# Expert rows of a mixture of experts in 25 whole tiles and 11 tiles of two 64-row units, instead of 39 whole tiles

## The reference

```python
gate = rmsnorm(x) @ wg_W + wg_b + (genre_embed @ gg_W + gg_b)
gate_w = softmax(gate)
topk_w, topk_i = top_k(gate_w, 2)
h1 = relu(x @ W1[e] + b1[e])       # 256 -> 512, for each expert e
h2 = relu(h1 @ W2[e] + b2[e])      # 512 -> 512
out_e = h2 @ W3[e] + b3[e]         # 512 -> 256
out = sum over the token's two experts of weight * out_e
```

## Time and profile before

| | us |
|---|---|
| time of the kernel, median of 3 runs | 798.35 (797.91 to 800.69) |
| the profiled execution, its own time | 798.27 |
| its span in the profile | 796.5 |
| PE busy | 753.0 (95%) |
| DVE busy | 496.9 (62%) |
| ACT busy | 278.9 (35%) |
| POOL busy | 80.9 (10%) |
| granted TensorE clock, mean | 0.979 |

### The profile page before, as it was taken

How to read it: one execution, slowest core, us unless ns; L and a number is a source line. 1 busy time by engine, 2 the same in 40 slices (tenths; PEclk the granted TensorE clock), 3 DMA queues, 4 the chain that set the end, 5 groups by cost and what they waited for, 6 DMA issues and landing times.

```text
span 796.5 us, 23084 instructions
## 1 busy us (share of the span) xinstructions
PE 753.0 (95%) x9468; PEld 657.4 (83%) x9468; DVE 496.9 (62%) x1090; ACT 278.9 (35%) x838; POOL 80.9 (10%) x91
## 2 busy tenths in 40 slices
PE   4489999999999999979999999999999999999786
PEld 2389989999999999967778878977897789778675
DVE  4664574444444445235688778777877787778756
ACT  3022212212211221234446435633563455336420
POOL 2221101111111100010000000000000000000000
PEclk8699999999999999989999999999999999999989
DMA  9878343111111113200000000000000000000000
GB/s 321 278 253 266 118 180 100 34 35 41 40 35 34 41 29 106 74 28 21 22 22 10 28 28 16 16 29 28 9 21 29 28 9 21 29 8 15 8 9 15
DMA packets 29686, 48.53 MB, mean 61 GB/s; under 512 B 3307, under 2 KB 19435, under 8 KB 29069
## 3 DMA queue, kind: packets, MB, share of 16 engines
q1 hardware_dynamic: 20432, 32.47, 12.0%
q0 software_dynamic: 3408, 9.31, 4.0%
q10 hardware_dynamic: 5741, 5.27, 2.0%
HBM read 39.82 MB, written 7.22 MB: 59 GB/s over the span
## 4 chain that ended last, share of the span: by engine, by line
PE 88%; DVE 6%; ACT 1%; issue 1%; another core or an unknown queue 1%; DMA 1%; POOL 1%; DVEq 0%; ACTq 0%; POOLq 0%
PE ps L611 17%; PE ps L686 15%; PE ps L600 8%; PE ps L623 8%; PE ps L763 7%; PE ps L709 7%; PE ps L731 4%; PE ps L783 3%; PE ps L754 2%; PE ps L724 2%; PE ps L814 2%; PE ps L795 2%; PE ps L861 2%; PE ps L829 2%; PE ps L878 2%; PE ps L851 1%
## 5 line engine op out<-in xcount | busy, mean ns | idle before, releaser
L611 PE MATMUL ps<-h_t,w_now 128*128 128x128 f32 x1248 | 145.9, 275 | 1.0 <-DVE h_t L1322 1.0
L611 PEld LDWEIGHTS ps<-h_t,w_now 128*128 128x128 f32 x1248 | 142.4, 192 | 1.5 <-issue 1.4
L686 PE MATMUL ps<-arena,l_weights 128*128 128x128 f32 x1024 | 128.5, 280 | 0.5 <-ACT arena L1017 0.5
L686 PEld LDWEIGHTS ps<-arena,l_weights 128*128 128x128 f32 x1024 | 122.0, 195 | 2.0 <-ACT arena L1017 0.9
L979 ACT ACTIVATE h_t<-ps,cols 128x128 f32<-128x128 f32 x156 | 44.4, 367 | 215.0 <-PE ps L600 187.0
L1313 DVE COPY w_now<-arena 128x2048 f32 x39 | 47.8, 1227 | 104.5 <-PE ps L611 100.7
L1023 ACT ACTIVATE arena<-ps,cols 128x128 f32<-128x128 f32 x256 | 72.9, 370 | 20.8 <-PE ps L686 20.8
L600 PEld LDWEIGHTS ps<-xg_t,w_now 128*128 128x128 f32 x624 | 75.3, 192 | 4.8 <-DVE w_now L1305 2.1
L600 PE MATMUL ps<-xg_t,w_now 128*128 128x128 f32 x624 | 76.4, 276 | 2.3 <-ACT xg_t L970 2.0
L623 PE MATMUL ps<-arena,h_t 128*128 x312 | 73.8, 379 | 0.0
L495 POOL DMA_INDIRECT xg<-in_x,slot_tok x39 | 45.3, 1163 | 232.0 <-PE ps L590 204.3
(11 more groups left out here) (245 smaller groups left out, 1008.2 us busy)
## 6 DMA issues: line engine op xcount, KB each, us to landing
arena<-in_w SPq DMA_DIRECT2D x16, 512.0 KB
arena<-in_w SPq DMA_DIRECT2D x8, 1024.0 KB
expert_out<-y ACTq DMA_DIRECT2D x39, 128.0 KB
arena<-in_x_t SPq DMA_DIRECT2D x2, 1024.0 KB, 6.1
arena<-in_x SPq DMA_DIRECT2D x16, 128.0 KB, 2.5
out<-arena SPq DMA_DIRECT2D x16, 128.0 KB, 1.7
b<-in_b SPq DMA_DIRECT2D x1, 1024.0 KB, 13.5
l_weights<-in_wq SPq DMA_DIRECT2D x1, 1024.0 KB
```

The source lines that it names most:

```text
L611: last = mm(ps[:, 2, m * P:(m + 1) * P], w2_now[:, k, m * P:(m + 1) * P], h1_t[j % 2][:, k, :], start=k == 0, stop=k == KM - 1)
L686: last = mm(ps[:, b, c * P:(c + 1) * P], wt[:, k, f:f + P], m_t[:, k, :], start=k == 0, stop=k == KH - 1)
```

## The change

A slot list of 36 tiles takes the place of 39. 25 tiles (`FULL`) hold 128 rows of one expert each. What is left of each expert (under 128 rows) is padded to a multiple of 64 and goes to 11 mixed tiles (`MIXED`) of two 64-row units, each with an expert of its own. The mixed tiles stand at positions 10 to 20 of the order of work; 15 whole tiles follow them. `mixed(p)`, `nth(p)` and `slot_tile(p)` translate positions.

In a mixed tile the 64 rows of a unit are stationary and the weights move: the units occupy the two halves of the array's columns, and each half gets its own expert's weights. The result has rows on the partitions, so:

- PE has two more groups of four transposes in each mixed tile (`turn_h1`, `turn_h2`);
- DVE adds the bias as a row (`add_b1`, `add_b2`, 512 columns) before the transposes, and copies W1 and W2 twice, once for each unit; b1 and b2 rows come by two more indirect DMAs for each mixed tile, issued by POOL;
- ACT does both ReLUs as one instruction each after the transposes (`relu1`, `relu2_mixed`), and copies W3 twice (`take_w3`), 1024 columns each.

The extra buffers lie where the attention weights will be, so these are now loaded only after the last mixed tile. DVE's planning has more arithmetic, part of it issued without a wait after each instruction (`step.go`), and side stage 1 on DVE has eight more small instructions. In whole tiles too, DVE now waits for PE first and then fetches the expert number.

```diff
-SLOT_TILES = (TOPK * TOK + EXP * (P - 1)) // P
+UNIT = 64
+UNITS = P // UNIT
+FULL = -(-(TOPK * TOK - EXP * (P - 1)) // P)
+MIXED = -(-(TOPK * TOK - FULL * P + EXP * (UNIT - 1) - (UNIT - 1)) // P)
+SLOT_TILES = FULL + MIXED
+FIRST_MIXED = EXP + 2
+LAST_MIXED = FIRST_MIXED + MIXED - 1
...
+            sp.wait_ge(y_ps, LAST_MIXED + 1)
             for dst, name in ((wq, "wq"), (wk, "wk"), (wv, "wv"), (wo, "wo")):
...
             def layer1(j):
...
+                if mixed(j):
+                    for k in range(KH):
+                        for g in range(UNITS):
+                            part_ = slice(g * UNIT, (g + 1) * UNIT)
+                            last = mm(ps[part_, 0, :], xg_t[:, k, part_], w1_of[g][:, k, :],
+                                      start=k == 0, stop=k == KH - 1, tile_position=(0, g * UNIT))
+                    last.then_inc(l1_ps, 1)
+                    return
...
+            def turn_h1(j):
+                pe.wait_ge(h1r_set, nth(j) + 1)
+                if nth(j):
+                    pe.wait_ge(h1t_set, j)
+                for m in range(KM):
+                    last = pe.transpose(ps[:, 1, m * P:(m + 1) * P], h1_rows[:, m * P:(m + 1) * P], ident[:, :])
+                last.then_inc(h1r_turned, 1)
...
             def layer3(j):
...
+                if mixed(j):
+                    pe.wait_ge(h2m_set, nth(j) + 1)
+                    pe.wait_ge(y_set, j)
+                    pe.wait_ge(w3_set, nth(j) + 1)
...
+                if mixed(j - 1):
+                    turn_h2(j - 1)
                 if exists(j, SLOT_TILES):
                     layer2(j)
+                if mixed(j + 1):
+                    turn_h1(j + 1)
...
+            def relu2_mixed(j):
+                act.wait_ge(h2r_turned, nth(j) + 1)
+                act.wait_ge(y_ps, j - 1)
+                f(h2_t[j % 2][:, :, :], ps[:, 3, :].rearrange("p (k q) -> p k q", k=KM), ACT.Relu).then_inc(h2m_set, 1)
+
+            def take_w3(j):
...
+                act.wait_ge(y_ps, j)
+                for g in range(UNITS):
+                    e = act.value_load(row_expert[g * UNIT:g * UNIT + 1, nth(j):nth(j) + 1], min_val=0, max_val=EXP - 1)
+                    at = act.snap(e * E_SIZE + W3_AT)
+                    last = act.copy(w3_now[g].rearrange("p k n -> p (k n)"), arena[:, bass.ds(at, KM * HID)])
+                last.then_inc(w3_set, 1)
+
             def expert_step(j):
-                if exists(j + 1, SLOT_TILES):
+                if mixed(j - 1):
+                    take_w3(j - 1)
+                if exists(j + 1, SLOT_TILES) and not mixed(j + 1):
                     relu1(j + 1)
                 if exists(j + 2, SLOT_TILES):
                     copy_x(j + 2)
+                if mixed(j - 1):
+                    relu2_mixed(j - 1)
+                if mixed(j + 1):
+                    relu1(j + 1)
...
             def take_w1(j):
+                if j:
+                    dve.wait_ge(l1_ps, j)
+                if mixed(j):
+                    if nth(j) == 0:
+                        dve.wait_ge(setup_done, 1)
+                        dve.wait_ge(fa_stored, 16)
+                        dve.wait_ge(moe_loaded, 48 * EXP)
+                    for g in range(UNITS):
+                        at = dve.snap(unit_expert(j, g) * E_SIZE + W1_AT)
+                        last = dve.tensor_copy(w1_of[g][:, :, :].rearrange("p k n -> p (k n)"), arena[:, bass.ds(at, KH * MID)])
+                    last.then_inc(w1_set, 1)
+                    return
                 e = expert(j)
                 at = dve.snap(e * E_SIZE + W1_AT)
                 dve.wait_ge(moe_loaded, 48 * (e + 1))
-                if j:
-                    dve.wait_ge(l1_ps, j)
...
+                if mixed(j + 1):
+                    add_b1(j + 1)
                 if exists(j + 2, SLOT_TILES):
                     take_w1(j + 2)
...
+                if mixed(j):
+                    add_b2(j)
                 if exists(j + 1, SLOT_TILES):
                     take_w2(j + 1)
-                if exists(j, SLOT_TILES):
+                if exists(j, SLOT_TILES) and not mixed(j):
                     relu2(j)
```

More of the change, by code:

```diff
@@ L81, in exists, with mixed, nth, slot_tile @@
     return not isinstance(t, int) or 0 <= t < n
+def mixed(p):
+    return FIRST_MIXED <= p <= LAST_MIXED
+def nth(p):
+    return p - FIRST_MIXED if mixed(p) else p if p < FIRST_MIXED else p - MIXED
+def slot_tile(p):
+    return FULL + nth(p) if mixed(p) else nth(p)
 def later(t):
@@ L97, in __call__, with go, done @@
         self.n += 1
+        self.engine.wait_ge(self.sem, self.base + self.n)
+    def go(self, instruction):
+        instruction.then_inc(self.sem, 1)
+        self.n += 1
+    def done(self):
         self.engine.wait_ge(self.sem, self.base + self.n)
@@ L216, in build @@
         f_hid = r(KH, BATCH)
-        f_a, f_b, f_c = (r(HID, parts=BATCH) for _ in range(3))
+        f_a, f_b = (r(HID, parts=BATCH) for _ in range(2))
         f_s = r(8, parts=BATCH)
@@ L1254, in _ @@
-            tt(back, rest, first_slot, ALU.subtract).then_inc(dve_step, 1)
-            step.n += 1
-            step(tt(picked, rank, rest, ALU.subtract))
-            step(stt(picked, picked, float(P), back, ALU.is_lt, ALU.mult))
-            step(tt(rank, rank, picked, ALU.subtract))
-            for c in range(TOPK):
-                step(tt(picked, rank, mask[c], ALU.mult))
-                step(red(slot_f[:, c, :], picked, X, ALU.add))
+            first_row, seg_of = excl[:, :, 0], [seg[:, n * EXP:(n + 1) * EXP] for n in range(3)]
@@ new lines, in _ @@
+            from_of = [seg_from[:, n * EXP:(n + 1) * EXP] for n in range(3)]
+            step(tt(count_i, incl[:, :, TT - 1], first_row, ALU.subtract))
+            step.go(ts(full_i, count_i, -P, None, ALU.bitwise_and))
+            step(ts(up_i, count_i, float(UNIT - 1), None, ALU.add))
+            step.go(ts(seg_of[0], full_i, float(P), None, ALU.min))
+            step(ts(up_i, up_i, -UNIT, None, ALU.bitwise_and))
+            step.go(tt(seg_of[1], full_i, seg_of[0], ALU.subtract))
+            step(tt(seg_of[2], up_i, full_i, ALU.subtract))
@@ new lines, in _ @@
+            step.go(tt(to_rest, to_rest, jump, ALU.subtract))
+            step(tt(over_first, over_first, per_e(to_full), ALU.mult))
+            step.go(tt(over_full, over_full, per_e(to_rest), ALU.mult))
+            step(tt(rank, rank, over_first, ALU.add))
+            step(tt(rank, rank, over_full, ALU.add))
+            for c in range(TOPK):
+                step.go(tt(picked[c], rank, mask[c], ALU.mult))
+            step.done()
+            for c in range(TOPK):
+                step.go(red(slot_f[:, c, :], picked[c], X, ALU.add))
@@ L1326, in add_b3 @@
             def add_b3(j):
+                if mixed(j):
+                    dve.wait_ge(y_ps, j + 1)
+                    dve.wait_ge(y_stored, 16 * j)
+                    for g in range(UNITS):
+                        part_ = slice(g * UNIT, (g + 1) * UNIT)
+                        e = dve.value_load(row_expert[g * UNIT:g * UNIT + 1, nth(j):nth(j) + 1], min_val=0, max_val=EXP - 1)
+                        last = tt(y[part_, :], ps[part_, 4, 0:HID], b3[part_, bass.ds(e * HID, HID)], ALU.add)
+                    last.then_inc(y_set, 1)
+                    return
                 e = expert(j)
```

200 lines of the change are left out of this document (160 added, 40 removed).

## The result

The changed kernel takes 800.81 us (median of 20 runs, 799.66 to 804.06), the kernel before on the same chip 798.62 (20 runs): a ratio of 1.0029, 95% interval 1.0019 to 1.0040. It is 0.3% slower, 2.2 us, where 1.8 us less had been forecast. The profiled execution took 800.11 us with a span of 798.4. The time lies inside the range of 790.5 to 802.5 us that was given; the direction is the other. Where two times are compared in us without a word on how, the difference is that of the medians.

The account below looks back on a forecast made before the run. PE was taken to bound the kernel, the expert stage being PE alone. The terms -21.9 + 13.9 + 2.9 + 2.3 + 1.0 = -1.8 us on 798.27 us gave 796.5 us, range 790.5 to 802.5.

Parts of the forecast that it names:

- three whole tiles: Expert stage, bound by PE alone: three tiles fewer at 7.30 us each, -21.9 us.
- 11 mixed tiles: PE in mixed tiles: 8.56 us each, 1.26 more than a whole one, +13.9 us (10.6 to 17.4).
- fetch behind the wait, second copies: DVE's W1 and W2 copies, where PE already waits for DVE: +2.9 us, between 0 and 4.
- leaving the mixed tiles: Last mixed tiles: ACT's queue delays mixed ReLU 2, so PE waits before layer 3, +1.1 and +1.2: 2.3 us (0 to 3).
- planning: DVE's planning before the first expert tile: net +1.0 us, of it 1.7 for sixteen instructions without a wait; -0.7 to +3.9.
- the first W1: DVE's first copy of W1, with its fetch now behind the wait: +0.15 us.
- In step 9 W2 is copied twice ahead of ReLU 2 ... +0.5: First mixed layer 2: ReLU 2 ready 4.8 us after the previous layer 2, against PE's 4.3: +0.5 us.
- rival of an array that empties fully at each change: Changes between tiled and full products on PE drain the array: +13.2 us, 809.7 us; chance 0.005.
- Step 0: First expert step: ReLU 2 delayed by the fetch +0.75, first W1 +0.15, together 0.9 us.
- Costs nothing in steady state: Whole tiles: the fetch behind the wait delays ReLU 2 by 0.75 us, inside DVE's spare 0.93, so no cost.
- ACT did not set the pace of the mixed tiles: Rival: ACT's chain from store to ReLU 2 paces mixed tiles; 804.2 us at 1.0 us more; chance 0.11.
- The waits did not find cover: Rival: the waits are hidden, leaving three tiles, mixed tiles and planning: -7.0 us, 791.3 us; chance 0.28.

Follow-up runs that it names:

- tiles_37: The kernel before with 37 tiles instead of 39, leaving out two tiles empty for this input: 785.69 us, 0.9825 of the kernel before.
- three_fixes: Changed kernel with expert number fetched before the wait, mixed ReLU 2 first on ACT, mixed tiles at 14 to 24: 791.65 us, 0.9904 of the kernel before.
- after_again: The changed kernel, unchanged, run again on a second chip: 796.48 us against 795.25 for the kernel before, 1.0007.
- before: The kernel before, unchanged, on the chip of the result: 798.62 us.
- before_again: The kernel before, unchanged, for a second profile, on the second chip: 795.23 us in one run, against a median of 795.25.
- after: The changed kernel in its first measurement, that of the result: 800.81 us, 1.0029 of the kernel before.
- after_third: The changed kernel, unchanged, on a third chip: 800.77 us against 799.65 for the kernel before, 1.0027.
- after_fourth: The changed kernel, unchanged, on a fourth chip: 802.32 us, 1.0036 of the kernel before.
- after_fifth: The changed kernel, unchanged, as a control in a later set of runs: 796.08 us against 796.30 for the kernel before, 0.9993.
- after_sixth: The changed kernel, unchanged, as the control on a further chip: 795.62 us against 796.52 for the kernel before, 0.9983.
- fetch_first: The changed kernel with the expert number fetched before the wait on PE, for W1 and W2: 792.82 us, 0.9964 of the kernel before.
- at_14_again: The changed kernel with mixed tiles at positions 14 to 24, repeated in a later set of runs: 793.89 us, 0.9969 of the kernel before.
- the edit that it implied: The changed kernel with ACT's mixed ReLU 2 ahead of the next whole tile's ReLU 1 and the copy of x: 798.46 us, 0.9989 of the kernel before.
- mixed_at_14: The changed kernel with mixed tiles at positions 14 to 24 instead of 10 to 20, third chip: 796.98 us, 0.9968 of the kernel before.
- the burst that was made on purpose twice: Changed kernel, mixed tiles at 14, POOL's first b1 gather held until layer 2 of tile 12: 793.12 us (0.9967), then 792.82 us (0.9952).
- before_wait_first: The kernel before with DVE waiting for PE first and fetching the expert number after, in both copies: 797.55 us, 1.0025 of the kernel before.
- warm_36: The changed kernel with 36 instead of 24 dummy matmuls at its start: 799.84 us against 800.02 for the kernel before, 1.0010.
- four_fixes: Changed kernel with fetch before wait, mixed ReLU 2 first, mixed tiles at 14, 36 dummy matmuls: 788.82 us, 0.9900 of the kernel before.

## Why the prediction was wrong

By its own steps, from profiles without the late release at the first mixed tile:

| step | forecast | measured | from |
|---|---|---|---|
| three whole tiles | -21.9 | -21.9 | `tiles_37`, 7.31 each |
| 11 mixed tiles | +13.9 | +14.8 | `three_fixes`, tiles 12 to 26 |
| fetch behind the wait, second copies | +2.9 | +3.4 | intervals of layer 2, below |
| leaving the mixed tiles | +2.3 | +2.6 | `three_fixes` against `after_again` |
| planning | +1.0 | +0.5 | gate to slot table, below |
| sum | -1.8 | -0.6 | |

On these three chips the ratios mean +0.6, -0.6 and -1.4 us, each with an interval of about 1 us or more to either side; their average of -0.5 agrees with the sum, but doesn't prove it. On the other three they mean +2.2 to +2.9 us. The profiles allow a sharper comparison, since the span can be cut at the gate's first result, the first layer 2 and the first attention scores (times in us):

| profile | to the gate's result | to the first layer 2 | to the first scores | to the end |
|---|---|---|---|---|
| `before` | 13.5 | 32.0 | 296.4 | 454.6 |
| `before_again` | 13.5 | 31.8 | 296.4 | 451.6 |
| `after` | 15.7 | 32.6 | 297.5 | 452.6 |
| `after_third` | 15.9 | 32.7 | 297.5 | 452.7 |
| `after_fourth` | 16.2 | 32.0 | 299.3 | 454.8 |
| `after_again` | 16.3 | 31.3 | 296.9 | 451.4 |
| `after_fifth` | 16.0 | 32.8 | 295.5 | 451.2 |
| `after_sixth` | 15.6 | 31.2 | 295.5 | 451.7 |

All of the forecast but the planning (and 0.15 us for the first W1) lies in the column to the first scores: -21.9 + 13.9 + 2.9 + 2.3 = -2.8 us. Measured are -0.9 us (`after_fifth`, `after_sixth`; +0.4 in `after_again`, with its last interval of 9.02) without the late release and +1.1 (`after`, `after_third`) with it. The release is worth 2.0 us there and turns the sign of this stage. The profiled pair of the result, 1.9 us apart in span, is then 2.16 (slow first products) + 0.58 (planning and first tile) + 1.10 (expert stage) - 1.94 (attention stage). The last goes with the granted clock, which differs between executions of the same code: in the 12 us from the first scores it is 0.72 in `before` and in `after_fourth`, 0.86 in `after`, `after_third` and `before_again`.

**The step that failed** is "Together 0.9 + 2.0 = 2.9 us; between 0, if all of it found cover, and 4", in its last part, "In step 9 W2 is copied twice ahead of ReLU 2 ... +0.5". It took for granted that DVE resumes 0.40 us after PE's layer 2, so that the copy, with its fetch, starts at T + 1.15. So it does in `after_again` (T + 1.18), where PE's wait is 0.33 us against 0.5 forecast. But in half of the sets of runs, that of the result among them, the copy starts at T + 3.07 and PE waits 2.20 us. Of the 4.0 us by which the forecast was off, 1.9 are this; the rest is in sizes, below, and in what varies from execution to execution. The rows of before had a warning that I quoted for another purpose: the group of line 1045 in the earlier trace rows shows "remote 6.2" of idle time on ACT. That is this kind of lateness, at the start of the attention stage. It cost the kernel before 1.7 us (3.11 against 1.38 us of waiting on PE in `before` and `before_again`), and I didn't ask whether the change could meet another.

The other sizes, in the order of the sum:

- *Mixed tiles.* The steady tile is right (8.56 forecast, 8.56 to 8.57 measured). The 0.9 us more are the passages between tiles of the two kinds, for which I used the steady price. The prediction's rival of an array that empties fully at each change would have cost 13.2 us more; these runs have room for less than 1, so for this kernel it is out. The Trainium skill, "TensorEngine Tiling (Array Packing)", section "Key Properties", says that a change of the tiling mode drains TensorE; whatever drain there is, is in the 0.16 us of the earlier trace rows.
- *Fetch behind the wait, second copies.* The fetch's part is shown by two opposite edits. Step 0 cost 0.6 (0.9 forecast). Behind the side stages the intervals of layer 2 to tiles 8, 9 and 10 grew by 0.5, 1.7 and 1.15 us, of which 1.0 belongs to the mixed tiles themselves: 2.4 against 2.0. Between `after_again` and `fetch_first` the three shrink by 0.8, 0.05 and 0.4, so the fetch accounts for about half of the 2.4. The rest is the second copies while DVE is late from the side stages: in `at_14_again`, with the mixed tiles elsewhere, the intervals to tiles 9 and 10 are back at 7.38 and 7.32 us. The last step of the stage added 0.4 (1.7 in one execution), and I had counted nothing for it. "Costs nothing in steady state" was right, but the last steps are not steady: DVE has the attention stage's work in them.
- *Leaving.* Named with its place and cause, and removed by the edit that it implied.
- *Planning.* Sized too high. The slot table, before and after:

```profile
31.97 0.20 DVE L1282 CAST slot_tok<-ps 128x39 int32<-128x39 f32 x1 [0.29 <-PE ps L570]
```

```profile
34.61 0.20 DVE L1453 CAST slot_tok<-ps 128x36 int32<-128x36 f32 x1 [0.35 <-PE ps L643]
```

From the gate's first result that is 31.97 - 13.52 = 18.45 us and 34.61 - 15.68 = 18.93: 0.5 us. It is the same in every other profile (18.92 to 18.95 with the change, 18.45 and 18.46 before). Sixteen instructions without a wait cost less than the 1.7 us that I took. The first layer 1, forecast about 1 us later, came at 42.41 instead of 39.75, 2.7 us later, but 2.2 of these are the slow first products.

Two rivals are decided. ACT did not set the pace of the mixed tiles; it has the 0.2 us to spare. The waits did not find cover, and `fetch_first` shows what it would have been worth.

**What stays open.** Why a release comes late at these two places on some chips was not settled: in `mixed_at_14`, on such a chip, the first mixed layer 2 has no such wait, so it hangs on the place or on what goes on beside it, and the burst that was made on purpose twice met chips that don't show it. With 1.9 us added to -0.6 the sum is +1.3, against +2.2 to +2.9 measured there. Two things that the sum doesn't hold can fill the gap in some executions, but how often is not shown: the clock that fell behind the late release in `after_fourth` (1.7 us), and the slow first products, if the change makes them likelier.

## What to carry to other kernels

A queue that waits first and fetches its address afterwards pays for the fetch wherever the other engine is already waiting for it: put the fetch ahead of the wait, and look for the price at the edges of a stage rather than in its steady state. A new kind of tile costs its steady price plus its edges: here, even without the late release, the waits at entry and exit (some 1.9 and 2.6 us) and the passages (0.9 us) together ate most of the 8 us that the tiles themselves won (21.9 - 13.9), and moving the seam away from the busy side stages and reordering one engine's queue gave the waits back. For a change worth under 1%, compare on more than one chip before a sign is believed.

## What the runs showed of the hardware

- The releases above: the same program has ACT and DVE resume some 2 us later in three of six sets of runs, always at the same places, with the granted clock at 1.00 until PE goes on. One release more in the changed kernel is 1.9 us of the 2.9 by which the ratios of the two kinds differ.
- Behind a wait of PE the granted clock can fall to 0.50 and stay there for some us: 0.50 from 346.20 to 352.20 in `before`, behind its 3.11 us at the start of the attention stage, from 346.33 to 348.33 in `before_again`, behind 1.38 us, and not at all in `before_wait_first`, behind 1.36. It is not the same in each execution: behind the 2.2 us at the first mixed layer 2 it fell in `after_fourth` and in none of the five other profiles.
- The first real products ran at half their pace (8 records in 1.94 us instead of 1.06) in 13 of the 18 profiled executions with 24 dummy matmuls ahead and 1.4 to 1.6 us of idle time between, and in neither of the two with 36 (no idle time in `warm_36`, 0.77 us in `four_fixes`). It moves the gate's result by 1.1 to 2.8 us. The granted clock doesn't show it. The stretch from 5.60 to 7.40 us (busy time of PE, weight loads, DVE, ACT and POOL with counts, then the granted clock, DMA share and GB/s), before and after:

```profile
5.60:7.40 1.80, 1.67 (x16) 0.45 (x16) 0.46 (x1) 1.06 (x1) 0.08 (x1) 1.00 1.01 414
```

```profile
5.60:7.40 1.80, 1.70 (x8) 0.40 (x12) 0.00 (x0) 1.06 (x1) 0.17 (x2) 1.00 1.03 423
```

  1.00 in both, with twice the products in the one. That it is PE's clock, as my expectation for `warm_36` put it, is therefore not shown; what is shown is that it comes with the old start and the new, and that it was absent in five of 18 executions with 24 dummy matmuls too, so two without it are weak evidence for the 36.
- Pairs of 64-column products with different stationary rows and different weights in the two halves run side by side at the pace at which they do in `l1_v`, 8.56 us for a mixed tile as worked out from the earlier trace rows.
